# A 1024-element add per tile given to an adding DMA, and GpSimd's masks made a slot ahead

## What is computed

```
z   = einsum('bfd,bgd->bfgd', x0, xk)           # g: 39, then 128, then 128
xk' = einsum('bpd,pm->bmd', z.reshape(b, f*g, d), W)   # 128 maps
out = concat([x1, x2, x3], axis=1).sum(-1)      # (512, 384)
h   = relu([out, dense] @ W_top1 + b); h = relu(h @ W_top2 + b); y = h @ W_top3
```

## Time and profile before

| | us |
|---|---|
| median of 3 runs | 829.9 (829.66 to 834.03) |
| the profiled execution's own time | 828.44 |
| its span | 826.6 |
| busy PE / DVE / ACT / POOL | 700.3 / 622.2 / 492.1 / 243.1 |
| L548, the 1024-element add, 64 times | 78.4 |
| L373, POOL's masks, 64 times | 56.1 |

### The profile page before, as it was taken

How to read it: one execution, slowest core, us unless ns; L and a number is a source line. 1 busy time by engine, 2 the same in 40 slices (tenths; PEclk the granted TensorE clock), 3 DMA queues, 4 the chain that set the end, 5 groups by cost and what they waited for, 6 DMA issues and landing times.

```text
span 826.6 us, 12250 instructions
## 1 busy us (share of the span) xinstructions
PE 700.3 (85%) x3327; PEld 499.7 (60%) x3327; DVE 622.2 (75%) x1409; ACT 492.1 (60%) x1659; POOL 243.1 (29%) x247
## 2 busy tenths in 40 slices
PE   0007887988898999998899989988898999999977
PEld 0002554766575777765576667755576687666757
DVE  1004678999799966898899855897899966899970
ACT  0002555776677664766676544866677665867861
POOL 6740023331364060612182140532173100100100
PEclk9998799999999999999999999999999999999999
DMA  3710202120111112020202011020212011020000
GB/s 86 286 24 5 75 2 53 31 60 21 46 40 49 32 24 60 4 79 2 72 13 75 7 32 55 3 80 2 60 24 64 18 32 47 1 78 1 1 1 1
DMA packets 23422, 33.96 MB, mean 41 GB/s; under 512 B 7815, under 2 KB 10615, under 8 KB 22966
## 3 DMA queue, kind: packets, MB, share of 16 engines
q1 hardware_dynamic: 18230, 31.84, 12.5%
q0 software_dynamic: 5120, 1.29, 1.8%
HBM read 9.13 MB, written 0.00 MB: 11 GB/s over the span
## 4 chain that ended last, share of the span: by engine, by line
PE 54%; DVE 19%; issue 14%; ACT 6%; DMA 3%; SPq 2%; DVEq 1%; another core or an unknown queue 0%; ACTq 0%
PE x_ps L731 9%; DVE sums L615 8%; PE v_ps L706 6%; PE v_ps L708 6%; PE v_ps L707 6%; PE a_ps L708 5%; PE a_ps L706 5%; PE a_ps L707 5%; ACT scaled L413 4%; DVE scaled L554 4%; PE s_ps L757 4%; PE s_ps L829 3%; DMA b_sb<-a_sb 3%; DVE z_sb L588 2%; SPq L312 2%
## 5 line engine op out<-in xcount | busy, mean ns | idle before, releaser
L413 ACT ACTIVATE scaled<-a_ps,x0c 128x128 f32<-128x128 f32 x1216 | 350.3, 379 | 168.9 <-PE a_ps L708 158.6
L615 DVE SCALAR_TENSOR_TENSOR sums<-v_ps,x0c,sums 128x128 f32<-128x128 f32 x768 | 215.1, 342 | 14.0 <-PE v_ps L708 11.8
L706 PE MATMUL v_ps<-w_hi,x_hi 128*128 128x512 f32 x320 | 172.6, 539 | 20.3 <-DVE sums L615 16.4
L357 POOL DMA_INDIRECT e_sb<-in_tables,ids_now x140 | 157.9, 1128 | 40.5 <-issue 39.1
L373 POOL TENSOR_TENSOR diag_sb<-x0c,eye_sb 128x320 f32<-128x320 f32 x64 | 56.1, 879 | 366.0 <-PE s_ps L829 365.5
L731 PE MATMUL x_ps<-z_sb,w_sb 117*128 117x512 f32 (+1 forms) x210 | 112.7, 618 | 27.6 <-DVE e_parts L510 13.9
L707 PE MATMUL v_ps<-w_lo,x_hi 128*128 128x512 f32 x320 | 128.2, 400 | 0.0
L708 PE MATMUL v_ps<-w_hi,x_lo 128*128 128x512 f32 x320 | 128.0, 400 | 0.0
L706 PE MATMUL a_ps<-w_hi,x_hi 128*128 128x512 f32 (+1 forms) x320 | 124.2, 388 | 1.0 <-issue 1.0
L707 PE MATMUL a_ps<-w_lo,x_hi 128*128 128x512 f32 (+1 forms) x320 | 123.9, 387 | 0.0
L708 PE MATMUL a_ps<-w_hi,x_lo 128*128 128x512 f32 (+1 forms) x320 | 123.3, 385 | 0.0
(11 more groups left out here) (77 smaller groups left out, 675.0 us busy)
## 6 DMA issues: line engine op xcount, KB each, us to landing
b_sb<-a_sb SPq DMA_DIRECT2D x300, 78.0 KB
w_sb<-in_w SPq DMA_DIRECT2D x1, 2496.0 KB
e_sb<-in_tables,ids_now POOLq DMA_INDIRECT x140
s_sb<-in_w SPq DMA_DIRECT2D x2, 1024.0 KB
wt_sb<-in_wt SPq DMA_DIRECT2D x1, 768.0 KB
s_sb<-in_w SPq DMA_DIRECT2D x1, 512.0 KB
wt_sb<-in_wt SPq DMA_DIRECT2D x1, 512.0 KB
w_raw<-in_w0a SPq DMA_DIRECT2D x1, 409.5 KB
```

The lines of the kernel that those rows point to most:

```text
L357: pool.indirect_dma_start(out=e_sb[0:rows, i, :], out_offset=None, in_=tables, in_offset=bass.IndirectOffsetOnAxis(ap=ids_now[0:rows, 0, i ...
L413: last = nc.scalar.activation(scaled[:, s % 2, to, j, :], bank[:, j * MAPS:(j + 1) * MAPS], ACT.Copy, scale=x0c[:, k % 4, s, lo + j:lo + j ...
L615: nc.vector.scalar_tensor_tensor(out=sums[:, s % 2, j, :], in0=v_ps[n % 2][:, j * MAPS:(j + 1) * MAPS], scalar=x0c[:, k % 4, s, lo + j:lo ...
L706: nc.tensor.matmul(to, high, w_high, start=True, stop=False)
```

## The change

Step 0 of `sum_tile` is taken out of DVE's program. In its place POOL waits for ACT's fourth scaled part and issues a DMA that adds parts 2, 3 into parts 0, 1 in SBUF (`halve`, 128 rows of 1024 float32, 512 KB). A tiny POOL add (`pace`, 1x2) stands ahead of the DMA and carries the wait. DVE's step 2 waits for that DMA (semaphore `halved`), and makes the 896-element add then. Part 1 and part 0 are added to `sums` separately in step 3, and step 4 has both folds. DVE's operations after the 1024-element one keep their sizes: 896, 512, 512, 256, 128.

The masks get eight buffers (two slots of four) and are made in the slot of their own tile, at h = 5s + 2, a slot before PE uses them; `halve` stands at h = 5s + 4. To make room, `z_first`, which is used only at the start, now lies in `scaled`.

```diff
-        diag_sb = sb("diag_sb", [128, 2, SB, F0 + 1])
+        diag_sb = sb("diag_sb", [128, 2, SUBS, SB, F0 + 1])
...
+            def mask(t, k, s):
+
+                tile = tile_of(t, k, s)
+                if s == 0:
+                    pool.wait_ge(x0c_ready, 4 * t + k + 1)
+                if not isinstance(t, int) or 4 * t + k >= 2:
+
+                    pool.wait_ge(s_done, tile - 2 * SUBS + 1)
+                nc.gpsimd.tensor_tensor(
+                    diag_sb[:, k % 2, s, :, :],
...
+                    ALU.mult).then_inc(diag_ready, 1)
+
+            def halve(t, k, s):
+
+                tile = tile_of(t, k, s)
+                if not isinstance(tile, int) or tile > 0:
+                    pool.wait_ge(paced, tile)
+                pool.wait_ge(scaled_ready, SCALED * tile + 4)
+                nc.gpsimd.tensor_tensor(pace[0:1, 1:2, 0:2], table_rows_sb[0:1, :, 0:2], table_rows_sb[0:1, :, 0:2],
+                                        ALU.add).then_inc(paced, 1)
+                part = scaled[:, s % 2, :, :, :]
+                pool.dma_start(part[:, 0:2, :, :].rearrange("p g f m -> p (g f m)"),
+                               part[:, 2:4, :, :].rearrange("p g f m -> p (g f m)"),
+                               accum_op=ALU.add).then_inc(halved[s % 2], 16)
...
+                    if exists(t, k) and h % GROUPS == 2:
+                        mask(t, k, h // GROUPS)
+                    if exists(t, k) and h % GROUPS == GROUPS - 1:
+                        halve(t, k, h // GROUPS)
...
-                if step == 0:
-                    dve.wait_ge(scaled_ready, SCALED * tile + 4)
-                    nc.vector.tensor_tensor(part[:, 0:2, :, :], part[:, 0:2, :, :], part[:, 2:4, :, :],
-                                            ALU.add).then_inc(tail_step, 1)
-                if step == 1:
-                    dve.wait_ge(tail_step, TAIL * tile + 1)
+                if step == 2:
+
+                    dve.wait_ge(halved[s % 2], adds_of(t, k, s))
                     dve.wait_ge(scaled_ready, SCALED * tile + SCALED)
                     flat = part.rearrange("p g f m -> p (g f) m")
                     nc.vector.tensor_tensor(flat[:, 0:4 + LAST_A, :], flat[:, 0:4 + LAST_A, :],
                                             flat[:, 16:20 + LAST_A, :], ALU.add).then_inc(tail_step, 1)
+                if step == 3:
+                    dve.wait_ge(tail_step, TAIL * tile + 1)
+                    dve.wait_ge(macs, mac_count(tile, GROUPS - 2, 3))
+                    nc.vector.tensor_tensor(acc, acc, part[:, 1, :, :], ALU.add).then_inc(tail_step, 1)
                     dve.wait_ge(tail_step, TAIL * tile + 2)
-                    nc.vector.tensor_tensor(part[:, 0, :, :], part[:, 0, :, :], part[:, 1, :, :],
-                                            ALU.add).then_inc(tail_step, 1)
-                if step == 2:
+                    nc.vector.tensor_tensor(acc, acc, part[:, 0, :, :], ALU.add).then_inc(tail_step, 1)
+                if step == 4:
                     dve.wait_ge(tail_step, TAIL * tile + 3)
...
                     nc.vector.tensor_tensor(acc[:, 0:2, :], acc[:, 0:2, :], acc[:, 2:4, :],
                                             ALU.add).then_inc(tail_step, 1)
```

More of the change, by code:

```diff
@@ L40 @@
 SCALED = GROUPS + 1
-TAIL = 5
+TAIL = 4
 W1_PIECES = [(0, 4), (4, 8), (8, 10)]
@@ L119, in dlrm_tower @@
         eye_sb = sb("eye_sb", [128, 128 + SB])
-        mask = eye_sb[:, 128:128 + SB]
+        x2_mask = eye_sb[:, 128:128 + SB]
         w0_sb = sb("w0_sb", [3 * F0, T0, MAPS])
@@ L145, in dlrm_tower @@
         z0_sb = sb("z0_sb", [3 * F0, 2, COLS])
-        z_first = sb("z_first", [3 * F0, T0, COLS])
         w0_raw = sb("w0_raw", [3 * F0, 2, T0, MAPS])
@@ L151, in dlrm_tower @@
         scaled = sb("scaled", [128, 2, SCALED, 4, MAPS])
+        z_first = scaled.rearrange("p a g f m -> p (a g f m)")[0:3 * F0, 0:T0 * COLS]\
+            .rearrange("p (i c) -> p i c", c=COLS)
         sums = sb("sums", [128, 2, 4, MAPS])
-        pace = sb("pace", [128, 1, FH], i32)
+        pace = sb("pace", [128, 2, FH], i32)
         x2t = sb("x2t", [128, 2, SUBS, MAPS])
-        diag_sb = sb("diag_sb", [128, 2, SB, F0 + 1])
+        diag_sb = sb("diag_sb", [128, 2, SUBS, SB, F0 + 1])
         s_sb = sb("s_sb", [128, 4 * FG, BT])
@@ L214, in dlrm_tower @@
         scaled_ready = sem("scaled_ready")
+        halved = [sem("halved0"), sem("halved1")]
+        paced = sem("paced")
         tail_step = sem("tail_step")
@@ L265, in mlp_step, with adds_of @@
             return None, None
+        def adds_of(t, k, s):
+            return 16 * SUBS // 2 * 4 * t + 16 * (SUBS // 2 * k + s // 2 + 1)
         def tile_of(t, k, s):
@@ L365, in slot @@
                         pool.wait_ge(ids_moved, 2 * t + (k + 3) // 2)
[L366 to L377, removed]
+                    if exists(t, k) and h % GROUPS == 2:
+                        mask(t, k, h // GROUPS)
+                    if exists(t, k) and h % GROUPS == GROUPS - 1:
+                        halve(t, k, h // GROUPS)
                     if k % 2 == 1 and h == GATHER_AT + 1 and exists(t, k + 3):
-                        nc.gpsimd.tensor_tensor(pace[:, :, :], table_rows_sb[:, :, :], table_rows_sb[:, :, :],
+                        nc.gpsimd.tensor_tensor(pace[:, 0:1, :], table_rows_sb[:, :, :], table_rows_sb[:, :, :],
                                                 ALU.add)
```

12 lines of the change are left out of this document (4 added, 8 removed).

## The result

The changed kernel takes **894.2 us** in the median (4 runs, 891.36 to 898.24) against 830.46 (829.66 to 834.03) for the kernel before beside it: ratio **1.0778, 95% interval 1.0732 to 1.0823**. The forecast was 817.5, with 801 to 845 as its range. The profiled execution took 898.24, with a span of 896.4.

A forecast was written before the change was run, and what follows sets the result against it. It took PE and DVE, equally loaded in lockstep, as the bound. Terms -30.3 + 9.6 + 6 + 2.4 = -12.3 us took the profiled 828.44 to 816.1, stated as 817.5 for the median, range 801 to 845.

The forecast's parts named there:

- the one on DVE's add: In each slot DVE loses the 1024-element add, 4.9 us; PE's waits for DVE's sums and splits go, 30.3 us less.
- the first two waits: PE's waits for sums that free a v_ps bank, 16.4 us, and behind DVE's bf16 splits, 13.9 us.
- the text's first step: What bounds the kernel: DVE in the last slot, PE and DVE in lockstep in an ordinary odd slot.
- the DMA beside the shifts: At slot starts the last tile's adding DMA meets SP's shifts: 0.5 us later at 12 starts, 6 us more.
- the bubble: PE idle at 12 slot starts while DVE awaits the shifts: 22.8 us in place of 13.2, 9.6 more.
- a rival too: At the 15 slot starts, shifts come 1.5 us later and take the whole gain: 829 us, no change; chance 0.14.
- L: Time from ACT's fourth part to DVE's being let into the 896-element add: 4.2 to 5.9 us, taken as 5.0.
- The masks, "gives nothing by itself": On POOL, masks a slot ahead drop the two-buffer wait for PE's products; needed for a timely DMA, no gain counted.
- the tail: At the very end nothing hides the DMA: PE's last x2 product 8.4 us after ACT's fourth part, 2.4 us more.
- the likeliest rival, a late landing: DVE waits for the adding DMA ahead of the sums of group 2: 853 us as a median, slower; chance 0.22.

The follow-up runs named there:

- e8: The kernel before, in its own order, with DVE's 1024-element add cut to 16 elements and no DMA: 850.74 us, ratio 1.0226.
- e9: The kernel before with DVE's last split steps at half steps 8, 10, 12 and PE's turns at 15 and 17: 813.92 us, ratio 0.9798.
- e4: The changed kernel with ten idle products on PE ahead of each slot's first z_sb product: 880.28 us, 1.0592 of the kernel before.
- e2: The changed kernel with each slot's last tile added on DVE at step 0, three adding DMAs left: 839.44 us, 1.0101 of the kernel before.
- e5: The changed kernel with a plain copy of the same 512 KB in place of the adding DMA: 846.61 us, 1.0193 of the kernel before.
- e10: The kernel before with masks a slot ahead, and POOL still held at the old four places by the old waits: 842.16 us, ratio 1.0109.
- e1: The kernel before with only the masks made a slot ahead and z_first in scaled: 861.69 us, ratio 1.035.
- e7: The changed kernel with all 1024-element adds on DVE at step 0 and no adding DMA: 840.92 us, 1.0114 of the kernel before.
- e15: The kernel before with splits a half step earlier, PE's turns one later, and the add cut to 16 elements: 859.76 us, ratio 1.0349.

## Why the prediction was wrong

**The step that failed** is the one on DVE's add: "A slot's 38.1 us of DVE go to 33.2, and PE is ahead as the bound by 5 us. DVE's splits and sums are then in time, and I count the first two waits as gone: 16.4 + 13.9 = 30.3 us less." Measured: 39.1 us of such waits where 30.3 had stood; with the add gone altogether and no DMA (e8) 30.2. I read a wait for DVE as a want of DVE's time. For the splits it was the place of the awaited instruction in DVE's order, which e9 showed: with the splits moved a half step earlier and PE's turns one later, the 13.9 us went and the kernel took 2% less, without any relief. For the sums' 16.4 us it is shown only that they don't depend on the add (16.4 in e8). With no gain in these waits only the costs were left, and they decide the sign.

The same misreading stands in the text's first step. "DVE is busy 23.72 of 24.00 us ... there DVE is the bound" leaves out that PE is busy 23.57 in that row. In e8 DVE lacks the add in these tiles too, and the last slot takes the same 35.9 us from its first sum to its last `x2t` as before.

**The term that was mis-sized** is the DMA beside the shifts, +6, with the bubble, +9.6. The meeting was foreseen, and it was a rival too, but at 1.5 us for each start. The first multiply came 2.4 us later than in the earlier trace rows, the `z_sb` waits grew by 33.5 us in place of 15.6, and the falls of the clock, which the sum put at nothing, came on top: 65 us more at 1.2 GHz, of which e4 got back 14 net. In all, e2 puts 55 us on the fourth adding DMA. The Trainium skill's rule on two source reads ("Collectives: The Full Stack", The bandwidth ceiling), was weighed in the text for L alone and not for the shifts beside it. It bears on them: with a plain copy of the same bytes (e5), half the engine time, 48 us of the loss are gone.

**The masks, "gives nothing by itself":** wrong by some 1% to 3.5% in the kernel without DMAs (e10, e1). The text saw that "the two-buffer wait for PE's products, which now held POOL, goes" and did not ask what that wait was holding back: the gathers. The earlier trace rows had it, 365.5 us of idle time on that line. In the changed kernel the adding DMAs' own waits for ACT pace POOL again (493.1 us), and its gathers run at most 7 us into the next slot, so less of it should apply there; how much, no run shows.

**Right:** L in the tail, 5.19 against 5.0, and in the median (the DMA's last packet ends 5.0 us behind ACT's fourth part), but it scatters, from 4.4 to 7.7, and is over 5.5 in 26 of 64 tiles, nearly all of them the first or last of a slot; the tail, +8.6 for +8.4. DVE waited for the DMA 7.3 us in all. So the likeliest rival, a late landing, was false: the kernel was slower, but at another place. DVE's busy time was forecast at 544 and is 579; some 20 us of the difference are in its last two adds of a tile, which take longer (see below).

## What to carry to other kernels

A wait of one engine for another is worth the time of the relief only if the awaited instruction is late because of load. Look at what stands ahead of it in its engine's order; moving that can be worth more than removing work. And before a wait is taken away, ask what that engine does next: here the masks' wait kept the gathers in the middle of a slot, and without it the kernel was 3.5% slower, with it 1.1%. A transfer that starts at the same moment as one on the critical path can push that one back (2.4 us at each start here), and if PE's idle time grows by it, the clock charges it again.

## What the hardware showed that was not expected

- An adding DMA from SBUF to SBUF took 2.03 times a plain copy's engine time (2889 and 1421 us for 33.5 MB), and its last packet ended 4.4 to 7.7 us behind ACT's fourth part (median 5.0).
- Shifts of 78 KB on another queue issued beside it: the first multiply begins 5.3 to 7.5 us after their source is ready, in place of 3.9 to 4.3 at all starts but one.
- Two adds of DVE took longer with the same shapes: 128x256 went from a mean of 479 to 666 ns and 128x128 from 286 to 409. This goes with the DMA and not with DVE's new order: in the same order without the DMA (e7) they take 443 and 305, with a plain copy in its place (e5) 648 and 401. In the changed kernel 39 of the 64 adds of 128x256 overlap POOL's issue of such a DMA, and they take 770 ns in the mean, the other 25 504. The rows of DVE by line and form, after, then e7:
```profile
L589 DVE TENSOR_TENSOR sums<-sums 128x256 f32<-128x256 f32 x64 | 42.6, 666 | 0.0
L595 DVE TENSOR_TENSOR x2t<-sums 128x128 f32<-128x128 f32 x64 | 26.1, 409 | 3.3
...
L591 DVE TENSOR_TENSOR sums<-sums 128x256 f32<-128x256 f32 x64 | 28.4, 443 | 0.0
L597 DVE TENSOR_TENSOR x2t<-sums 128x128 f32<-128x128 f32 x64 | 19.5, 305 | 3.3
```
- In some stretches with 15 to 18 gathers one behind the other, the results of PE came 5 to 10 us behind their records; in the one shown (e15) the DMA engines carried 0.05 of their load. The path is open.
